# Message layer of a graph network: a PSUM bank per slot for source rows and own rows, and a new table of step times

## The reference

```
msgs   = z[edge_dst] @ Wd + z[edge_src] @ Ws + edge_weight[:, None] * ww + bm
agg    = segment_max(msgs, edge_dst)            # 0 for nodes without an edge
hidden = relu(z @ W1a + agg @ W1b + b1)
x      = _layernorm(z + hidden @ W2 + b2)
```

## Time and profile before

| What | Before |
|---|---|
| median of 3 runs | 3875.34 us (3873.74 to 3887.8) |
| span of the profiled execution, first to last instruction | 3856.9 us |
| what lies around the span, taken as median less span | 18.4 us |
| message stage, first gather to the end of the span | 3247.0 to 3856.9, 610 us |
| mean granted TensorE clock, whole span | 0.885 |
| mean granted TensorE clock, message stage | 0.76 |

### The profile page before, as it was taken

The page is one execution under the profiler, slowest core; times in us unless marked ns, Lnnn a source line. Parts: engine busy times, 40 slices in busy tenths (PEclk is TensorE's granted clock), DMA queues, the critical chain, the costliest instruction groups (busy, mean ns, idle before and its releaser), DMA issues. The chain is left out here.

```text
span 3856.9 us, 54369 instructions
## 1 busy us (share of the span) xinstructions
PE 3033.4 (79%) x11490; PEld 2023.8 (52%) x11490; DVE 2725.5 (71%) x6900; ACT 2299.0 (60%) x5259; POOL 2523.9 (65%) x2721
## 2 busy tenths in 40 slices
PE   3124149999999998899979999979999996777676
PEld 2012035555555555777759999955555553343333
DVE  3005749999999998777769989969999994222222
ACT  2003039999999999777623333439999994232332
POOL 5750069999999998777534444436666763666665
PEclk7557569999999999899989999989999997777777
DMA  5012025555555554444323343322322321222221
GB/s 190 1 36 90 1 76 171 171 168 169 171 164 175 164 176 141 113 123 119 109 86 112 114 112 110 109 81 72 88 83 84 86 82 44 72 73 72 72 68 46
DMA packets 262118, 404.65 MB, mean 105 GB/s; under 512 B 61938, under 2 KB 104135, under 8 KB 262033
## 3 DMA queue, kind: packets, MB, share of 16 engines
q1 hardware_dynamic: 204920, 304.18, 24.6%
q0 software_dynamic: 44032, 73.90, 8.4%
q10 hardware_dynamic: 13081, 25.69, 2.0%
HBM read 213.15 MB, written 194.37 MB: 106 GB/s over the span
## 5 line engine op out<-in xcount | busy, mean ns | idle before, releaser
L256 POOL TENSOR_TENSOR dn_rstd<-dn_var,w_minus_half 128x4 f32<-128x4 f32 x294 | 292.6, 1002 | 16.7 <-DVE dn_var L241 16.5
L1603 POOL DMA_INDIRECT m_src<-table_x,e_src_first x196 | 191.1, 975 | 127.5 <-issue 52.1
L1603 POOL DMA_INDIRECT p_src<-table_x,e_src x196 | 213.1, 1087 | 93.0 <-issue 53.6
L2491 POOL DMA_INDIRECT out_rows<-m_x,e_out_first x196 | 197.6, 1008 | 94.0 <-issue 65.8
L648 POOL DMA_INDIRECT scratch_node_row<-o_own,e_out x196 | 192.0, 979 | 90.7 <-issue 62.4
L1643 POOL DMA_INDIRECT g_own<-in_x,e_dst x196 | 223.9, 1142 | 36.9 <-issue 36.9
L2576 DVE TENSOR_TENSOR m_y<-m_bout,m_own 128x512 f32<-128x512 f32 x49 | 33.9, 692 | 294.3 <-DMA a_typ<-in_type_row 166.3
L1603 POOL DMA_INDIRECT a_src<-table_x,e_src x196 | 200.9, 1025 | 47.6 <-issue 37.5
L1634 POOL DMA_INDIRECT g_src<-scratch_wide,e_src x196 | 192.0, 980 | 58.8 <-issue 46.0
L1409 PE MATMUL n_banks<-w_gru_both,d_xT 128*128 128x256 f32 x784 | 223.6, 430 | 8.6 <-ACT d_xT L1446 8.6
L1409 PEld LDWEIGHTS n_banks<-w_gru_both,d_xT 128*128 128x128 f32 x784 | 192.9, 327 | 71.3 <-ACT d_xT L1446 68.6
(11 more groups left out here) (486 smaller groups left out, 9952.8 us busy)
## 6 DMA issues: line engine op xcount, KB each, us to landing
table_x<-d_x SPq DMA_DIRECT2D x294, 256.0 KB, 2.0
g_src<-in_x_wide SPq DMA_DIRECT2D x97, 262.0 KB
scratch_wide<-g_src SPq DMA_DIRECT2D x97, 262.0 KB
out_rows<-d_x SPq DMA_DIRECT2D x97, 256.0 KB
s_x<-in_x ACTq DMA_DIRECT2D x31, 768.0 KB
table_x<-d_xT SPq DMA_DIRECT2D x49, 256.0 KB
scratch_post<-d_x SPq DMA_DIRECT2D x49, 256.0 KB, 2.0
p_rc<-scratch_rcount SPq DMA_DIRECT2D x49, 256.0 KB
```

Source lines behind the costliest of these rows:

```text
L256: pool.tensor_tensor(self.rstd[s][:], self.var[s][:], minus_half[:], ALU.pow).then_inc(self.rooted[s], 1)
L1603: pool.indirect_dma_start(out=self.rows[s][:, t * P:(t + 1) * P], out_offset=None, in_=self.table, in_offset=bass.IndirectOffsetOnAxis(ap= ...
L2491: pool.indirect_dma_start(out=D["out"], out_offset=bass.IndirectOffsetOnAxis(ap=Ed.out_first[:, at:at + 1], axis=0), in_=x4[s][:, t * P:(t ...
```

## The change

Source rows and own rows get a bank for each slot, so all eight are in use, and two waits look at the step's own slot, two groups back, in place of the group before. The table is replaced.

```
-    bank_src, bank_own = mem.ps("m_bsrc"), mem.ps("m_bown")
-    bank_hid, bank_out = ([mem.ps(f"m_b{n}{s}") for s in range(S)] for n in ("hid", "out"))
+    bank_src, bank_own, bank_hid, bank_out = ([mem.ps(f"m_b{n}{s}") for s in range(S)] for n in ("src", "own", "hid", "out"))
...
-    AT = (0, 2.5, 5.1, 7.6, 5.6, 6.1, 11.7, 14.2, 14.9, 17.1, 12.2, 14.7, 16.8, 18.6, 19.8, 22.9, 25, 25.9, 28.5, 29.4, 29.8,
-          33.3, 41.9, 44.4, 47, 49.5)
-    PERIOD = 10.2
+    AT = (0, 2.57, 5.14, 7.71, 1.7, 1.9, 11.9, 12.85, 13.6, 15.8, 11.2, 13.5, 15.7, 17.3, 18.5, 19.3, 21.6, 22.5, 23.3, 24.5,
+          24.8, 25.8, 27, 29.6, 32.2, 34.75)
+    PERIOD = 10.3
...
                 if k == TURN_SRC:
                     gsrc.arrived(pe, i, s)
-                    wait(pe, scanned[s - 1], before(i, s))
-                    transpose_tiles(pe, bank_src, src[s], W.ident).then_inc(src_turned[s], 1)
+                    wait(pe, scanned[s], i)
+                    transpose_tiles(pe, bank_src[s], src[s], W.ident).then_inc(src_turned[s], 1)
...
                 if k == TURN_OWN:
                     wait(pe, own_loaded[s], 16 * i + 16)
-                    wait(pe, own_copied[s - 1], before(i, s))
-                    transpose_tiles(pe, bank_own, own[s], W.ident).then_inc(own_turned[s], 1)
+                    wait(pe, own_copied[s], i)
+                    transpose_tiles(pe, bank_own[s], own[s], W.ident).then_inc(own_turned[s], 1)
```

More of the change, by code:

```diff
@@ L2509, in step @@
                     wait(pe, row_loaded[s], 32 * i + 32)
-                    pe.matmul(bank_src[:], W.msg_src[:], srcT[s][:], start=True, stop=False)
-                    pe.matmul(bank_src[:], W.msg_w[:], wrow[s][:], start=False, stop=True).then_inc(made[s], 1)
+                    pe.matmul(bank_src[s][:], W.msg_src[:], srcT[s][:], start=True, stop=False)
+                    pe.matmul(bank_src[s][:], W.msg_w[:], wrow[s][:], start=False, stop=True).then_inc(made[s], 1)
                 if k == TURN_OWN:
                     wait(pe, own_loaded[s], 16 * i + 16)
-                    wait(pe, own_copied[s - 1], before(i, s))
-                    transpose_tiles(pe, bank_own, own[s], W.ident).then_inc(own_turned[s], 1)
+                    wait(pe, own_copied[s], i)
+                    transpose_tiles(pe, bank_own[s], own[s], W.ident).then_inc(own_turned[s], 1)
                 if k == OWN:
@@ L2536, in step @@
                     wait(act, made[s], i)
-                    act.copy(srcT[s][:], bank_src[:]).then_inc(src_copied[s], 1)
+                    act.copy(srcT[s][:], bank_src[s][:]).then_inc(src_copied[s], 1)
                 if k == COPY_OWN:
@@ L2540, in step @@
                     wait(act, own_made[s], i)
-                    act.copy(ownT[s][:], bank_own[:]).then_inc(own_copied[s], 1)
+                    act.copy(ownT[s][:], bank_own[s][:]).then_inc(own_copied[s], 1)
                 if k == RELU:
@@ L2569, in step @@
                     wait(dve, hidden[s], i)
-                    dve.tensor_tensor_scan(backward(mx[s]), backward(low[s]), backward(bank_src), mx[s - 1][:, 0:1],
+                    dve.tensor_tensor_scan(backward(mx[s]), backward(low[s]), backward(bank_src[s]), mx[s - 1][:, 0:1],
                                            ALU.add, ALU.max).then_inc(scanned[s], 1)
```

## The result

The changed kernel takes 3941.33 us (median of 4 runs, 3940.81 to 3943.54) against 3876.0 us of before on the same chip: a ratio of 1.0166, 95% interval 1.0145 to 1.0187. It is slower by 65 us, where 3940 us were forecast.

The account below looks back on a forecast made before the run. The loop through PE was taken to set the 11.96 us per group, POOL having 1.6 us to spare. Open trips to ACT gave +67 us, all else 0: 3856.9 + 67 = 3924, plus 18.4 is 3942, said as 3940; range 3800 to 4010.

Parts of the forecast that it names:

- Banks and waits: Waits of TURN_SRC and TURN_OWN on the other slot were already over by program order: gain 0, bounds 0 and 0.
- A turn at full clock: One whole turn of PE's loop per group at 2.4 GHz: 9.63 us, where it was 7.49.
- The trips to ACT: HIDDEN-RELU-PRODUCT and TURN_SRC-COPY_SRC-SOURCE lose PRODUCT's cover: 1.4 us more per group, +67 us (bounds +50 and +84).
- the sum over the two gaits: One full-clock and one slow turn per pair of groups: 13.0 to 13.7 us per group, middle 13.35.
- SCAN behind SUM and NEWTON: On DVE, NEWTON is through before SCAN can start: cost 0, with 0.5 us of cover.
- Stores: On POOL, stores two segments earlier use up its slack but don't set the pace: cost 0, at most 1.6 us per group.
- The clock: PE's mean clock in the message stage: 0.7 to 0.77, with PE's busy time near 435 us.
- the rule of the Trainium skill: PE's small idle times between groups of matmuls swing its clock; three short waits per turn would lower it further.
- POOL waiting more for transposes: Expected sign in the changed kernel's trace: more of POOL's waiting ended by PE's transposes; 51.7 us before.
- B: Rival: PE's clock falls more, at 0.65 15.7 us per group, +180 us, 4055 us; chance 0.09.
- C: Rival: PE's signals come on time, clock stays up, POOL sets the pace: 3797 us, or 3834 at 0.9; chance 0.29.
- D: Rival: PE's standing goes, clock stays at 0.76, nothing to be measured: 11.9 us per group, 3872 us; chance 0.12.

Follow-up runs that it names:

- banks_only: Changed kernel's banks and waits with the table of the kernel before; ratio to before 0.9999.
- later_store: Changed kernel with only its four stores moved back to four segments behind the first gather, as in the kernel before; ratio to before 1.0089.
- order_back_late: order_back with its four stores one more segment later, four behind the first gather as in the kernel before; ratio to before 0.9992.
- product_end: Kernel before with one edit: PRODUCT(k) moved to the end of its segment, behind RELU(k); ratio to before 1.0031.
- product_back: Changed kernel with one edit: PRODUCT(k-1) again between the transposes and SOURCE(k); ratio to before 1.0127.
- early_store: Kernel before with only the stores moved 7 us nearer to SCALE; ratio to before 1.0092.
- norm_behind: later_store with SQUARE(k-1) behind the two copies, SUM and NEWTON behind SCAN, and SCALE behind RELU; ratio to before 1.0054.
- order_back: Changed kernel with PRODUCT again between transposes and SOURCE, SQUARE behind the copies, SUM and NEWTON behind SCAN, SCALE behind RELU, stores one segment later; ratio to before 1.0048.
- warm8: Kernel before with 8 more bf16 matmuls per group that nobody reads, 4 ahead of SOURCE and 4 ahead of HIDDEN; ratio to before 1.0138.
- no_wrow: Kernel before without the product of the edge weights with ww, 2 matmuls per group; ratio to before 0.9966.
- late_store: Changed kernel with only its four stores 5 us later, all three segments behind the first gather; ratio to before 1.0095.

## Why the prediction was right, and where only the sum was

*Banks and waits, gain 0.* Right: banks_only, 0.9999.

*A turn at full clock, 9.63 us.* Right in its parts: 0.78 us idle ahead of PRODUCT, 2.14 us from PRODUCT to SOURCE, shortest distance of two scans 9.62 us (before 7.33). The rows of before held all of this. The waits themselves came in every group as forecast (49 times ahead of SOURCE, 49 ahead of PRODUCT), but were longer than 1.2 and 0.8 us: 110.8 and 57.8 us in all, with single ones of up to 8.6.

*The trips to ACT, +67 us.* Mis-sized. later_store has both trips bare and the norm's steps in the way, and nothing else of weight: 1.0089 of 3876 is 34 us (25 to 44). By the steps above these are 24 us for PRODUCT's place and 14 for the norm's, 38 together, since order_back_late at their end is 3 us under before. The step that failed is the sum over the two gaits: its lower end already let the standing swallow the waits of the slow turn and still gave +50, because it let every other group pay them in full. The standing swallows more than that. product_end points to it, with 86 us less of standing ahead of HIDDEN for 12 us more of time. The picture of two kinds of turn did not fit the rows of before either: 7.5 of 23.9 us at full clock and the rest at half would be a mean clock of 0.66, and the stage has 0.76. In the slow stretch of the earlier trace rows the clock is 1.00 while the matmuls start, and 0.55 in the mean while PE stands (columns as in the earlier trace rows):

```profile
3404.60:3410.00 5.40, 5.32 (x15) 2.75 (x15) 0.00 (x0) 1.98 (x6) 4.18 (x5) 1.00 0.18 53
3410.00:3416.80 6.80, 0.00 (x0) 0.00 (x0) 2.00 (x3) 0.63 (x1) 5.28 (x6) 0.55 0.33 91
```

*SCAN behind SUM and NEWTON, cost 0.* Not tested by itself. It is a part of the norm's place, 14 us together with SQUARE ahead of COPY_SRC.

*Stores, cost 0.* Wrong, and this is the main miss. The text had the fact in hand, "POOL's slack is gone", and priced it at 0 because a chain of 17 us per two groups is shorter than two turns. That was the chain at full clock with every signal in time. A signal that is late by 4 to 7 us would hold a store with no slack, and every gather behind it; that this is where the 30 us come from is argued, not shown, and product_back has the wait without late signals. Measured: 0.77% between later_store and the changed kernel, 30 us, and 36 us when put into the kernel before. The forecast was 67 + 0, the runs show 34 + 30 = 64 us (the 30 is what is left of 64, and early_store bears it out). So the forecast met the time by luck: one term was too large by about what the other lacked.

*The clock.* It fell to 0.70. The prediction gave 0.7 to 0.77 and expected PE's busy time to stay near 435 us; it is 495, since more of the same matmuls ran at the lower level: OWN's take 911 ns in the mean, where they took 716. The mean clock does not tell this by itself, since norm_behind has PE busy for 488 us in the stage at a clock of 0.74: before, PE spends part of its time at half clock standing idle. In one window, 3260 to 3820 us, product_end has 0.75, norm_behind 0.75, later_store 0.71, order_back 0.72 and the changed kernel 0.71, before 0.76. That bears on the rule of the Trainium skill ("TensorE: Matmul & The Clock Gate", section "A second HAM failure mode: psum-queue depth-cycling"): the bare waits alone, as in product_end and norm_behind, hardly moved the clock here. It fell in the changed kernel, as the rule has it, but also in order_back, where the trips are covered and not in early_store (0.75). So the rule's direction is right for the whole change; which waits lower the clock these runs don't show.

*POOL waiting more for transposes.* Wrong: it waits for scaled rows (165.6 us) and no longer for transposes.

*Rivals.* B, at 4055 with a clock below 0.68, did not come. C's idea, that short runs with waits between them would bring the signals in time, has a core: the standing ahead of HIDDEN did go, to 5.7 us, and PRODUCT's signal is over 2 us late in 9 groups, not 21. In product_end and later_store it is 3, in norm_behind 1, in product_back none. But none of these is faster than before: signals in time were worth no more than the waits that went with them, and a signal that is still late shows at another place, as the 6.98 us ahead of SOURCE above. D, that the standing goes and nothing can be measured, is nearly what product_end does.

## What to carry to other kernels

In a software pipeline don't price a tightened distance by a chain in which every signal is in time. Here a distance of 1 to 3 us of nominal time between SCALE and its store cost 0.6 to 0.9%, and one of 6 us nothing, on a queue, POOL's, that also issues the gathers. Compare the distance with the longest waits that the profile shows. A step of PE that lies between "write to PSUM" and "read back" is cover; before it is moved, look for what stood behind it, and for how long PE stands elsewhere in the same turn: that time can take up the new waits. And when an edit has several parts, a right total says nothing of its terms: time each by itself.

## What the runs showed of the hardware

PRODUCT's signal can come long after the modelled end of its last matmul: 3.8 us in the kernel before, 6.4 us in the changed one. How often depends on the order of steps. It is over 2 us late in 18 to 24 of 49 groups in before, banks_only, order_back_late, early_store, warm8 and no_wrow, in 10 in order_back, in 1 to 13 where PRODUCT stands at the end of the segment (norm_behind 1, late_store 13), and in none in product_back, each counted in one execution. Where it is late in the kernel before, PE mostly had no idle time ahead of PRODUCT; in the changed kernel it had 0.8 us and more each time. More matmuls, with the granted clock at 0.83, left it at 24 groups (before 21). What holds the signals back was not found.

In the stretch of the earlier trace rows the matmuls go on starting at the pace of full clock while PRODUCT's signal is still out, and then PE is shown idle for 6.9 us. It may still be at work there, which the profile can't tell; so PE's busy and idle times should not be read as its pace in such a stretch.
